# Differential attention and a switch FFN on one core: the products of probabilities with V in one run at place 5 of a head pair, the projections and V at places 7 to 3

## What is computed

```python
Q, K = X @ Wq + bq, X @ Wk + bk      # 16 heads, each 2 * 64 columns
V = X @ Wv + bv                      # 16 heads, 64 columns
A1, A2 = Q1 @ K1.T / 8, Q2 @ K2.T / 8
P = softmax(A1) - lam * softmax(A2)
O = P @ V
Y = layernorm(concat(O) @ Wo + bo) * gamma + beta, times 0.2
routes = argmax(softmax(t @ switch_w + switch_b))       # 8 experts
out = (gelu(t @ w1[e] + b1[e]) @ w2[e] + b2[e]) * max probability
```

## Time and profile before

| what | value |
|---|---|
| median of three runs | 1920.71 us |
| profiled execution, its own time | 1919.09 us |
| its span | 1917.3 us |
| PE busy | 1829.6 us, 95% |
| PEld busy | 1418.8 us, 74% |
| DVE busy | 1535.7 us, 80% |
| ACT busy | 1399.4 us, 73% |
| POOL busy | 705.9 us, 37% |
| DMA, mean | 233 GB/s, 446.07 MB |

### The profile page before, as it was taken

The page is one execution under the profiler, slowest core; times in us unless marked ns, Lnnn a source line. Parts: engine busy times, 40 slices in busy tenths (PEclk is TensorE's granted clock), DMA queues, the critical chain, the costliest instruction groups (busy, mean ns, idle before and its releaser), DMA issues. The chain is left out here.

```text
span 1917.3 us, 33022 instructions
## 1 busy us (share of the span) xinstructions
PE 1829.6 (95%) x10625; PEld 1418.8 (74%) x10625; DVE 1535.7 (80%) x2559; ACT 1399.4 (73%) x3286; POOL 705.9 (37%) x758
## 2 busy tenths in 40 slices
PE   5899999999999999999999999999988599999997
PEld 4677777777777777777777777777755499999896
DVE  7788888888888888888888888889967376666265
ACT  6788888888888888888888888887867376666100
POOL 2344223233223233233233233232246275555443
PEclk9999999999999999999999999999999799999999
DMA  9998988888888888888888888888894766666898
GB/s 290 267 247 241 238 227 231 224 226 227 228 229 228 213 227 230 225 228 232 222 227 232 226 226 228 215 226 226 219 167 97 250 216 235 238 228 207 297 382 284
DMA packets 230307, 446.07 MB, mean 233 GB/s; under 512 B 29090, under 2 KB 122064, under 8 KB 224144
## 3 DMA queue, kind: packets, MB, share of 16 engines
q1 hardware_dynamic: 225392, 434.02, 81.3%
q0 software_dynamic: 4768, 10.25, 1.8%
HBM read 184.34 MB, written 58.50 MB: 127 GB/s over the span
## 5 line engine op out<-in xcount | busy, mean ns | idle before, releaser
L581 ACT ACTIVATE e<-p_score,nmax 128x512 f32<-128x512 f32 x1024 | 698.6, 690 | 129.2 <-DVE nmax L802 129.0
L802 DVE TENSOR_REDUCE nmax<-p_score 128x2 f32<-128x1024 f32 x512 | 623.3, 1217 | 165.4 <-PE p_score L908 164.2
L437 POOL TENSOR_SCALAR e<-e,rrec,lam 128x512 f32<-128x512 f32 x512 | 395.8, 773 | 963.3 <-DVE rrec L762 962.9
L908 PE MATMUL p_score<-ks,qs 128*128 128x512 f32 x2048 | 580.5, 405 | 17.3 <-DMA ks<-k_parts 12.8
L908 PEld LDWEIGHTS p_score<-ks,qs 128*128 128x128 f32 x2048 | 366.0, 188 | 188.8 <-ACT e L581 54.2
L516 ACT COPY pT<-p_tr 128x512 f32<-128x512 f32 x512 | 301.3, 588 | 128.2 <-PE p_tr L920 124.8
L871 PE MATMUL p_proj<-xh,w 128*128 128x512 f32 x1024 | 387.1, 419 | 6.0 <-POOL xl L419 4.6
L769 DVE SCALAR_TENSOR_TENSOR pm<-e,rrec 128x512 f32<-128x512 f32 x512 | 391.5, 765 | 1.6 <-POOL e L437 1.5
L920 PE MATMUL p_tr<-consts,pm 128*128 128x128 f32 x2048 | 310.3, 274 | 3.3 <-ACT pT L516 3.2
L920 PEld LDWEIGHTS p_tr<-consts,pm 128*128 128x128 f32 x2048 | 250.5, 141 | 82.2 <-issue 19.2
L935 PE MATMUL p_pv<-pT,v 128*64 128x512 f32 x1024 | 250.5, 611 | 2.0 <-DVE oT L774 2.0
(11 more groups left out here) (153 smaller groups left out, 1845.2 us busy)
## 6 DMA issues: line engine op xcount, KB each, us to landing
ks<-k_parts SPq DMA_DIRECT2D x512, 256.0 KB, 4.8
qs<-q_parts SPq DMA_DIRECT2D x512, 128.0 KB, 5.5
w<-weight_parts_scratch SPq DMA_DIRECT2D x56, 1024.0 KB, 10.4
w<-in_w SPq DMA_DIRECT2D x46, 1024.0 KB, 7.4
oT_scratch<-oT SPq DMA_DIRECT2D x64, 512.0 KB, 6.0
op<-oT_scratch SPq DMA_DIRECT2D x32, 1024.0 KB, 9.2
wv<-weight_parts_scratch SPq DMA_DIRECT2D x56, 256.0 KB, 5.7
weight_parts_scratch<-w SPq DMA_DIRECT2D x8, 1024.0 KB, 6.0
```

What stands on the lines that cost most here:

```text
L437: nc.gpsimd.tensor_scalar(e2, e2, rrec[:, g % 4, 1:2], lam[:, 0:1], ALU.mult, ALU.mult).then_inc(s_e2, 1)
L581: nc.scalar.activation(ex[:, g % EX, m, :], p_score[g % 2][:, m, :], ACT.Exp, bias=nmax[:, g % 2, m:m + 1], accum_out=rsum[:, g % 4, m:m + ...
L802: vec.tensor_reduce(nmax[:, g % 2, :], p_score[g % 2][:, :, :], AXX, ALU.max, negate=True).then_inc(s_max, 1)
L908: last_op = nc.tensor.matmul(p_score[g % 2][:, m, :], qs[j][u][:, m, qt * P:(qt + 1) * P], ks[j][u][:, m, part, :], start=(part == 0), sto ...
```

## The change

The projections and V of the next pair are made at places 7, 0, 1, 2 and 3: k1 (for the next pair, as before) at 7, q0 at 0, k0 at 1, V at 2, q1 at 3. The products with V are made in one run of 16 records at place 5, for the pair before. Places 4 and 6 hold only scores and transpositions. The parts of a projection are still made one step later, for k1 therefore at place 0 of the next pair. The output is copied and stored at place 7, one pair earlier than its second half was before, and SP's store stands ahead of k1's copies and no longer behind k0's. The parts of V's weights are made for the pair three ahead, at places 5 and 6. Nothing is computed in another way.

```diff
--- before.py
+++ after.py
@@ -198,9 +198,13 @@
         RANK_PAIR = RANK_STEP // TPP
 
         ORDER = ("q0", "k0", "q1", "k1")
-        AT_STEP = {0: "q0", 2: "k0", 4: "q1", 6: "k1"}
-        V_STEP = 3
-        PV_FIRST, PV_LAST = 5, 1
+        AT_STEP = {0: "q0", 1: "k0", 3: "q1", 7: "k1"}
+        V_STEP, PV_STEP, O_STEP = 2, 5, 7
+
+        def made_before(g):
+
+            pair, st = divmod(g - 1, TPP)
+            return (pair + 1, AT_STEP[st]) if g >= 1 and st in AT_STEP and pair + 1 < NPAIRS else None
 
         def bank_of(pair, what):
 
@@ -360,8 +364,6 @@
                 if pair + 1 < NPAIRS:
                     for what in "qk":
                         spread(0, what, pair + 1)
-                if pair >= 2:
-                    store_o(pair - 2)
                 if pair % 2 == 0 and QT <= pair // 2 + 2 < ITERS:
                     load_wv(pair // 2 + 2)
                 if pair + 3 < PAIRS:
@@ -372,11 +374,12 @@
                     load_raw_v(pair + 4)
                 if pair + 2 < PAIRS:
                     store_w(pair + 2)
+                if pair >= 1:
+                    store_o(pair - 1)
                 if pair + 1 < NPAIRS:
                     spread(1, "k", pair + 1)
                 if PAIRS <= pair + 3 < NPAIRS:
                     load_w(pair + 3)
-            store_o(NPAIRS - 2)
             store_o(NPAIRS - 1)
             sp.wait_ge(s_ost, 16 * NPAIRS)
 
@@ -435,9 +438,11 @@
                 if g == 0:
                     pool.wait_ge(s_lam, 1)
                 nc.gpsimd.tensor_scalar(e2, e2, rrec[:, g % 4, 1:2], lam[:, 0:1], ALU.mult, ALU.mult).then_inc(s_e2, 1)
+                if g == 1:
+                    low_v(2)
+                if st == 6 and pair + 3 < PAIRS:
+                    low_v(pair + 3)
                 if pair + 2 < PAIRS:
-                    if st == 1:
-                        low_v(pair + 2)
                     if st == 3:
                         low_qk(pair + 2, 0)
                     if st == 5:
@@ -563,11 +568,10 @@
 
             for g in range(STEPS):
                 pair, st = g // TPP, g % TPP
-                if st == 2 and pair >= 2:
-                    copy_o(pair - 2)
-                what = AT_STEP.get(st - 1)
-                if what and pair + 1 < NPAIRS:
-                    high_part(pair + 1, what)
+                if made_before(g):
+                    high_part(*made_before(g))
+                if st == O_STEP and pair >= 1:
+                    copy_o(pair - 1)
                 if g >= LAG:
                     copy_pT(g - LAG)
                 for m in range(2):
@@ -584,9 +588,11 @@
                 if g == EXP_STEP:
                     act.wait_ge(s_rd, SHIFTED)
                     nc.scalar.activation(exr[:, :, :], lg[:, :, :], ACT.Exp).then_inc(s_re, 1)
+                if g == 0:
+                    high_v(2)
+                if st == 5 and pair + 3 < PAIRS:
+                    high_v(pair + 3)
                 if pair + 2 < PAIRS:
-                    if st == 0:
-                        high_v(pair + 2)
                     if st == 1:
                         scale_q(pair + 2)
                     if st == 2:
@@ -595,7 +601,6 @@
                         high_qk(pair + 2, 1)
             for g in range(STEPS - LAG, STEPS):
                 copy_pT(g)
-            copy_o(NPAIRS - 2)
             copy_o(NPAIRS - 1)
 
         @block.vector
@@ -801,17 +806,16 @@
                 dve.wait_ge(s_score, g + 1)
                 vec.tensor_reduce(nmax[:, g % 2, :], p_score[g % 2][:, :, :], AXX, ALU.max,
                                   negate=True).then_inc(s_max, 1)
-                what = AT_STEP.get(st - 1)
-                if what and pair + 1 < NPAIRS:
-                    low_part(pair + 1, what)
+                if made_before(g):
+                    low_part(*made_before(g))
                 if g >= 2:
                     combine(g - 2)
                 if g == 2:
                     add_bv(0)
                 if st == V_STEP + 1 and pair + 1 < NPAIRS:
                     add_bv(pair + 1)
-                if st == 2 and pair >= 2:
-                    low_o(pair - 2)
+                if st == O_STEP and pair >= 1:
+                    low_o(pair - 1)
                 for _ in range(ROUTE_OPS[g - ROUTE_FROM] if 0 <= g - ROUTE_FROM < len(ROUTE_OPS) else 0):
                     next(route_on)
             assert next(route_on, "over") == "over"
@@ -819,7 +823,6 @@
                 reciprocals(g)
             combine(STEPS - 2)
             combine(STEPS - 1)
-            low_o(NPAIRS - 2)
             low_o(NPAIRS - 1)
 
         @block.tensor
@@ -920,22 +923,20 @@
                     last_op = nc.tensor.transpose(p_tr[:, k, :], pm[:, g % 4, k * P:(k + 1) * P], ident)
                 last_op.then_inc(s_tr, 1)
 
-            def times_v(pair, key_tiles):
+            def times_v(pair):
                 j, it = pair % 2, pair // 2
-                if key_tiles[0] == 0:
-                    pe.wait_ge(s_pT, (pair + 1) * TPP)
-                    pe.wait_ge(s_v, 2 * it + 2)
-                    if pair + 2 < NPAIRS and with_logits(pair + 2):
-                        pe.wait_ge(s_v, pair + 3)
-                    if pair >= 1:
-                        pe.wait_ge(s_olo, pair)
-                for k in key_tiles:
+                pe.wait_ge(s_pT, (pair + 1) * TPP)
+                pe.wait_ge(s_v, 2 * it + 2)
+                if pair + 2 < NPAIRS and with_logits(pair + 2):
+                    pe.wait_ge(s_v, pair + 3)
+                if pair >= 1:
+                    pe.wait_ge(s_olo, pair)
+                for k in range(QT):
                     for u in range(2):
                         c = j * P + u * D
                         last_op = nc.tensor.matmul(p_pv[u * D:(u + 1) * D, :], v[it % 2][:, k, c:c + D],
                                                    pT[j][u][:, k, :], start=(k == 0), stop=(k == QT - 1))
-                if key_tiles[-1] == QT - 1:
-                    last_op.then_inc(s_pv, 1)
+                last_op.then_inc(s_pv, 1)
 
             pe.wait_ge(s_const, 16)
             transpose_x(0)
@@ -956,10 +957,8 @@
                 scores(g)
                 if g >= LAG:
                     transposes(g - LAG)
-                if st == PV_FIRST and pair >= 1:
-                    times_v(pair - 1, (0, 1))
-                if st == PV_LAST and pair >= 2:
-                    times_v(pair - 2, (2, 3))
+                if st == PV_STEP and pair >= 1:
+                    times_v(pair - 1)
                 if g == RANK_STEP:
                     ranks()
                 if st in AT_STEP and pair + 1 < NPAIRS:
@@ -968,10 +967,9 @@
                     values(0)
                 if st == V_STEP and pair + 1 < NPAIRS:
                     values(pair + 1)
-            times_v(NPAIRS - 2, (2, 3))
             for g in range(STEPS - LAG, STEPS):
                 transposes(g)
-            times_v(NPAIRS - 1, range(QT))
+            times_v(NPAIRS - 1)
 
 
 def ffn_and_output_stage(nc, ins, xn_d, token_d, ys_d, oT_d, consts, tile_expert, slot_u, prob, out):
```

## The result

Four runs of the changed kernel gave a median of 1945.41 us (1944.66 to 1948.94), four of the kernel before 1919.97; the ratio is 1.0136 [1.0121, 1.0152]. So it is slower by 1.4%, where 1% less was predicted, and above the range. The profiled execution took 1945.01 us, its span is 1943.2 against 1917.3, so 25.9 more.

What follows compares the result with a forecast made beforehand. TensorE was taken to set the period. Terms -20.7 + 5 + 1.7 + 0.3 - 4 - 4 = -21.7 us gave 1897.4 us profiled, 1899.0 as a median; range 1889 to 1921, the forecast's own 1892 to 1909.

Steps and rivals of the forecast that it cites:

- The seams: TensorE, pairs 2 to 62: one run of products instead of two halves saves 0.34 us a pair, -20.7 us in all.
- Rival B: Products with V: the run costs 2 x 1.87, seams aren't saved; about -1 to -3, near 1919 us; chance 0.05.
- VectorE and ScalarE: Scores wait for exponentials of two places before; margins of 0.2 to 0.3 us hold, so nothing booked.
- Rival C: VectorE or ACT binds behind the run; with 0.2 us a pair lost, 1911 us; chance 0.15.
- k1's copies, with the store ahead: SP's queue: k1 there at 10.6 us after place 0, due at place 4 at 11.07, leaving 0.45.
- k0's copies: SP's queue: k0 there at 20.9, 4.0 behind the weights, due 21.77; 0.08 us a pair booked, +5 us.
- Rival A: Copies for k1 (place 4) or k0 (place 0) late, waits 20 us or more; 1937 us; chance 0.12 slower, 0.08 partial.
- The ends: First pairs: V waits less for its weights' low part, -4 us; end: last run and output copy come earlier, -4 us.

Runs made afterwards that it cites:

- experiment 2: Changed kernel with the load of the next weights issued behind k0's copies, no longer ahead of those of q0 and k0: 1911.0 us, 0.995 to the kernel before.
- experiment 8: Experiment 2's kernel with the products with V in two halves again, at places 5 and 6: 1912.5 us, 0.997 to the kernel before.
- experiment 1: Kernel before with only the products with V put in one run at place 5, all else in the old order: 1975.97 us, 1.0283.
- 3: Changed kernel with k1 projected at place 6 instead of 7: 1971.46 us, 1.0259 to the kernel before; with experiment 2's load move too, 1945.19 us.
- 6: Changed kernel with V's weight loads behind q1's copies: 1931.52 us, 1.0079; with them in place but cut to a quarter: 1926.35 us, 1.0045 to the kernel before.
- experiment 5: Changed kernel with the store of o straight behind k1's copies instead of ahead of them: 2142.77 us, 1.1152 to the kernel before.
- 4: Changed kernel with the store of o back at its old place, behind k0's copies: 1998.11 us, 1.0389 to the kernel before.
- experiment 7: Kernel before with the load of the next weights moved behind k0's copies: 2009.76 us, 1.0482.

## Why the prediction was wrong

- **The seams (-20.7): right.** With copies in time (experiment 2) the medians of places 0 to 7 came out within 0.03 each, and undoing the run cost 0.31 to 0.33 a pair (experiment 8). Rival B is out. In the changed kernel place 0 has 2.84 in the mean where 2.75 was booked, some 5 us in 54 pairs. That the term isn't separable from the order was not said: by itself the run costs 55 us (experiment 1, against the kernel before on the same chip), by the prediction's own 2.48 a place, used there only for the new order. (By its own terms the lower end of the range is 1888, not 1889.)
- **VectorE and ScalarE (0): right.** Places 0 and 1 are not longer than a projection makes them where copies are in time, and edit 2 takes 21.78 a pair. Rival C came true only in experiments 1 and 3, with other orders.
- **k1's copies, with the store ahead: right, against its small spare of 0.45.** From pair 7 to 55 place 3 lasts 2.80 in the mean, so k1 costs at most 0.05 a pair.
- **k0's copies (+5): this step failed.** The prediction put them "4.0 behind" the weights, "0.9 to spare". In the pair shown the weights landed at 17.2, 0.3 late, and k0 was there 5.9 behind them, at 23.1: 2.2 later than forecast and 1.3 later than due. Of the 1.9 in the 4.0, 0.7 was in the trace of before. Its 4.8 to landing is a median over k1's and k0's copies together, and k0's, which follow the weights, are the slower ones. The last of them in the old pair, issued at 924.30 (count, size, us to landing):

```profile
ks<-k_parts SPq DMA_DIRECT2D x1, 256.0 KB, 5.9
```

So it landed at 930.2, 4.7 behind the weights, which took 10.11 from 915.39 to 925.50. In the median of 44 old pairs k0's set took 7.8 us from its first issue, where 7.2 was booked, and k1's 6.75; the median of the landing behind the weights was 4.8. With 4.8 for the 4.0, the sum gives 21.7 against 21.77 due: no spare at all. The other 1.2 is new. In the old pair k0's copies are issued 7.07 behind the weights (915.39 to 922.46); now it is 5.43 (911.98 to 917.41), and V's weights and q1 follow at once (920.74, 923.64). The time that a transfer takes was carried over as a constant, though what is in flight beside it had changed. Taking neighbours away made k0 earlier: the weights (experiment 2, all of it) and three quarters of V's bytes (6, from 0.97 to 0.43 in the pairs with them); and putting the store nearer made it later (5). By the Trainium skill (DMA: Bandwidth & Descriptors, Queues, rings and completion order) each DMA engine consumes its descriptors in ring order, but a later one may finish its write before an earlier one. The first half, read as a strict order of service, would leave k0 untouched by V's load, which is issued behind it; the runs differ, by 0.5 us.
- **Rival A** came true by its own sign: waits for k of 20 us or more, and they were 20.8. It named the place, the mechanism and the threshold, and by its own formula the mean excess of (0.97 + 0.20) / 2 = 0.59 a pair gives 61 x (0.59 - 0.34) - 6 = +9; of the other 17 us, 11 are the first pairs and the end (+5.0 in the table, not -6), and the rest of the middle has 6, most of it place 0. It had a chance of 0.12, from spares worked out to 0.1 us on a landing time known to no better than a median over both sets of copies.
- **The ends (-4 - 4): half right.** The end itself gained what it should: the last output copy followed the last copy of transposed probabilities by 6.18 us instead of 11.30. The latter in the kernel before (its output copy, at 1493.47, is in the earlier trace rows), then both in the changed kernel:

```profile
1482.17 0.59 ACT L516 COPY pT<-p_tr 128x512 f32<-128x512 f32 x1 [1.27 <-PE p_tr L920]
```

```profile
1512.59 0.59 ACT L521 COPY pT<-p_tr 128x512 f32<-128x512 f32 x1 [1.27 <-PE p_tr L923]
1518.77 0.59 ACT L527 CAST oT<-p_pv 128x512 fp32r<-128x512 f32 x1 [5.59 <-PE p_pv L937]
```

But from place 5 of pair 62 to that last copy of probabilities it took 40.7 us instead of 34.0: the run in pair 62, and in pair 63 a wait of 3.1 us for late copies at place 4 that the kernel before does not have. So the stretch is 1.6 longer. In the first pairs V waited 3.5 for its weights instead of 5.0, but the scores at place 4 waited 7.3 us for copies over pairs 2 to 6, where before none of them waited for a copy: a gain of 4 was booked on TensorE alone, in a stretch where the copies now set the pace.

What stays open: pairs 61 and 62 are together some 5 to 18 us longer than two others of their kernel in all kernels, before included, while GpSimd scatters token numbers, and by how much differs from kernel to kernel (56.3 us for both before, 50.2 to 64.6 among the others). This moves the medians of two kernels apart by as much as most of the edits do, and it is why the stretches are compared here. That the scatters hold up the copies was only argued. How much of k0's delay the store ahead of k1 causes is open too, since experiments 4 and 5 brought waits of their own.

## What to carry to other kernels

A change of order on the engine that sets the pace moves every transfer with it: list for each DMA what is issued in the 10 us before and behind it, in the old order and the new, and take its landing time over only where these are alike. Take it from the very copies that have the deadline: a median over all copies of a kind mixes quick sets with slow ones (k1's 6.75 us and k0's 7.8 here). With the DMA engines at 0.86, a spare of 1 us on copies that take 7 to 8 was none. If such copies turn out late, move behind them the large loads that have a whole pair of slack. Splitting a load, so that each part goes out as late as its own user allows, is worth a trial, though its own gain isn't shown here. Here one load moved behind the copies was worth 35 us in the middle of the kernel, where the seams were worth 13 to 18; but a load is only moved safely in an order that still leaves it time (experiment 7).

## What the runs showed of the hardware

A transfer is delayed by one that is issued behind it on the same queue: k0's last copy had been issued before V's loads began, and the wait for it still fell from 0.97 to 0.43 us when these were cut to a quarter, while the pairs without such loads stayed at 0.20 to 0.25.

Copies of one kind and size can differ within each pair: in the kernel before the last of k1's four landed 4.9 us behind its issue, the last of k0's, issued behind the 1 MB of weights and q0's copies, 5.9 (medians).

The granted clock fell after a long wait. In experiment 5, stretches (last columns clock, DMA share, GB/s) and PE:

```profile
940.00:945.00 5.00, 4.32 (x12) 3.54 (x13) 2.21 (x3) 1.36 (x4) 0.00 (x0) 0.50 0.31 79
...
300.00:1300.00 1000.00, 884.26 (x4438) 639.48 (x4437) 739.25 (x1177) 708.84 (x1721) 256.08 (x345) 0.95 0.80 192
```

```profile
940.68 2.07 PE L911 MATMUL p_score<-ks,qs 128*128 128x512 f32 x4 [3.99 <-DMA ks<-k_parts]
...
945.85 1.09 PE L911 MATMUL p_score<-ks,qs 128*128 128x512 f32 x4
```

After a wait of 3.99 us the clock was 0.50, the lower of its two levels, between 940 and 945 us, the scores took 2.07 instead of 1.09, and the place 5.17 instead of 2.75. It recurs: in the 23 pairs between 8 and 57 whose place 7 was over 3.5 us too long, place 0 lasted 4.00 to 5.29, at a clock of 0.50 to 0.80 in its first 2.5 us. In the changed kernel, whose waits were at most 1.4 on PE between 300 and 1300 us, the clock stayed at 1.00. So this copy, late by some 4 us, cost 2.4 us more than its lateness, and experiment 5, at a mean clock of 0.95 in this stretch, lost by both.
